# Raw inputs projected and scaled afterwards in three layers, new fillers, halved value steps, and another order of tree rows

## The reference

```python
def _layernorm(x, axis=-1, eps=1e-05):
    m = jnp.mean(x, axis=axis, keepdims=True)
    v = jnp.var(x, axis=axis, keepdims=True)
    return (x - m) / jnp.sqrt(v + eps)
# l0a: linear attention with rotation and biases
q = (x @ Wq + bq); k = (x @ Wk + bk); v = (x @ Wv + bv)
q = _rope_apply(q, cos, sin); k = _rope_apply(k, cos, sin)
# l1x: softmax attention over the context, with mask; l2x: the same without mask
# l1a: relu attention
qkv = jax.nn.relu(jnp.einsum('bnc,oc->bno', x, qkv_weight))
vk = jnp.einsum('bnhe,bnhd->bhed', v_pad, k)
vk_q = jnp.einsum('bhed,bnhd->bnhe', vk, q)
proj_input = vk_q[..., :D] / (vk_q[..., D:] + EPS)
# l1f: four binary trees of depth 8 route each token to a leaf of its own
h = act(jnp.einsum('bsd,bsdl->bsl', x, w1[leaf]) + b1[leaf])
out = jnp.einsum('bsl,bsld->bsd', h, w2[leaf]) + b2[leaf]
# l1f: q, k, v = tree(xn); att = softmax(q @ k.T / sqrt(D)); y = xn + att @ v; y + tree_f(y)
# l3x: 16 heads of 64
q = _split_heads(x @ w_q)
dots = jnp.einsum('bhid,bhjd->bhij', q, k) * scale
attn = jax.nn.softmax(dots, axis=-1)
```

## Time and profile before

| | us |
|---|---|
| runs | 518.43, 514.8, 518.2; median 518.2 |
| the profiled execution | 517.47 |
| its span | 515.7 |
| TensorE busy | 471.1 (91%) |
| VectorE busy | 330.1 (64%) |
| ScalarE busy | 239.2 (46%) |
| GpSimd busy | 66.7 (13%) |
| mean granted clock of TensorE | 0.977 |

### The profile page before, as it was taken

The page is one execution under the profiler, slowest core; times in us unless marked ns, Lnnn a source line. Parts: engine busy times, 40 slices in busy tenths (PEclk is TensorE's granted clock), DMA queues, the critical chain, the costliest instruction groups (busy, mean ns, idle before and its releaser), DMA issues.

```text
span 515.7 us, 10193 instructions
## 1 busy us (share of the span) xinstructions
PE 471.1 (91%) x4120; PEld 388.0 (75%) x4120; DVE 330.1 (64%) x815; ACT 239.2 (46%) x480; POOL 66.7 (13%) x149
## 2 busy tenths in 40 slices
PE   8988999999875869899989899889999999999897
PEld 6857885555664868656557779769899899999797
DVE  5666579984745836898335464376777777755644
ACT  7223546777400434666733246275566565532131
POOL 1220124000016020200014005500000000001000
PEclk9989999999898898999999999899999999999999
DMA  7908301910177734000019000000000000019000
GB/s 261 396 3 175 74 1 41 208 22 1 30 282 255 291 93 159 1 1 0 2 60 390 3 1 1 2 0 1 1 0 2 1 1 1 1 42 417 34 1 5
DMA packets 9070, 42.05 MB, mean 82 GB/s; under 512 B 2287, under 2 KB 4919, under 8 KB 6327
## 3 DMA queue, kind: packets, MB, share of 16 engines
q1 hardware_dynamic: 7297, 32.73, 19.5%
q0 software_dynamic: 1728, 8.68, 4.6%
HBM read 34.72 MB, written 0.08 MB: 67 GB/s over the span
## 4 chain that ended last, share of the span: by engine, by line
PE 61%; DVE 18%; DMA 7%; issue 6%; POOL 4%; ACT 3%; SPq 1%; POOLq 0%; DVEq 0%; ACTq 0%
PE banks L281 55%; PE banks L284 6%; DVE peaks L1566 4%; DMA p_const<-in_const 3%; DMA region<-in_tree_v,leaf_no 2%; DMA region<-in_tree_f,leaf_no 1%; DVE probs L1563 1%; DVE small L2559 1%; POOL mv L386 1%; DVE probs L634 1%; DVE nmax L633 1%; DVE nmax L630 1%; DVE xnT L399 1%; ACT probs L655 1%; SPq L307 1%
## 5 line engine op out<-in xcount | busy, mean ns | idle before, releaser
L281 PE MATMUL banks<-identb 128*128 128x128 bf16 x944 | 69.2, 230 | 8.4 <-DMA region<-in_tree_q,leaf_no 3.9
L281 PEld LDWEIGHTS banks<-identb 128*128 128x128 bf16 x944 | 63.3, 104 | 11.4 <-DMA region<-in_tree_q,leaf_no 4.1
L1566 DVE TENSOR_REDUCE peaks<-banks 128x1 f32<-128x1024 f32 x56 | 66.5, 1220 | 4.2 <-PE banks L281 3.1
L2559 DVE TENSOR_REDUCE small<-banks 128x1 f32<-128x1024 f32 x32 | 39.1, 1222 | 24.3 <-PE banks L281 24.1
L2653 ACT CAST weights_hi<-banks 128x512 fp32r<-128x512 f32 x64 | 35.0, 590 | 27.4 <-PE banks L284 23.4
L284 PE MATMUL banks<-p_first,probs 128*128 128x128 f32 x320 | 44.2, 275 | 3.5 <-ACT probs L658 1.7
L2644 ACT ACTIVATE probs<-banks,nmax 128x1024 f32<-128x1024 f32 x32 | 35.6, 1115 | 24.5 <-DVE nmax L2563 24.4
L2569 DVE TENSOR_TENSOR weights_lo<-banks,weights_hi 128x512 fp32r<-128x512 f32 x64 | 41.4, 683 | 7.4 <-ACT weights_hi L2653 7.4
L284 PEld LDWEIGHTS banks<-p_first,probs 128*128 128x128 f32 x320 | 36.4, 140 | 10.6 <-ACT probs L655 2.3
L1650 ACT ACTIVATE region<-banks,seen 128x512 f32<-128x512 f32 x64 | 37.9, 702 | 12.2 <-PE banks L281 12.2
L1650 ACT ACTIVATE region<-banks 128x512 f32<-128x512 f32 x64 | 33.4, 606 | 17.1 <-PE banks L281 16.7
(11 more groups left out here) (493 smaller groups left out, 907.6 us busy)
## 6 DMA issues: line engine op xcount, KB each, us to landing
region<-in_w_l2f SPq DMA_DIRECT2D x1, 4096.0 KB, 15.4
region<-in_w_l3f SPq DMA_DIRECT2D x1, 4096.0 KB, 13.5
region<-in_w_b SPq DMA_DIRECT2D x1, 3076.0 KB, 14.7
values<-in_ctx SPq DMA_DIRECT2D x2, 1024.0 KB, 7.9
region<-in_w_l0f SPq DMA_DIRECT2D x1, 2048.0 KB, 21.7
keys_l1x<-shared SPq DMA_DIRECT2D x8, 256.0 KB, 4.1
keys_l2x<-probsT SPq DMA_DIRECT2D x8, 256.0 KB, 5.1
region<-in_w_l3d SPq DMA_DIRECT2D x1, 2048.0 KB, 17.0
```

What stands on the lines that cost most here:

```text
L281: return nc.tensor.matmul(o, lhsT, rhs, start=start, stop=stop)
L1566: nc.vector.tensor_reduce(peaks[:, h // 4 % 2, i:i + 1], ps[:, 2 * a:2 * a + 2, :], AX.XY, ALU.max, negate=True).then_inc(VM.sem, VM.now(( ...
L2559: return nc.vector.tensor_reduce(small[:, half:half + 1], ps[:, 2 * half:2 * half + 2, :], AX.XY, ALU.max)
```

## The change

In **l0a, l1a and l3x** the raw x is transposed and projected, not the normalised one. The mean is taken out of the weights ahead of time: with center = 1/128 - identity, the product center x W is the centred weight with its sign turned (l0x centres the weights of l0a and l1a, l1f those of l3x). The scale 1/sqrt(var + eps) comes in behind the projection: as a factor in the bias additions of l0a, in the relus and in the quotient of l1a, and in l3x in the maximum's factor and the exponential's scale, now a column (`rooted`) where it was the number 0.125. `late_plan`, `late_vector` and `late_tensor` take the place of the three `start_` functions there.

**Fillers:** 18 go in l0x; l1a has 7 for 19; l3x has 9, 7, 6 and 9 for 20, 3, 3 and 5; l1f has 32 more ahead of tree q; l2x has 22 more ahead of its first turned shift and 20 behind it. **l0a** moves the second block of keys behind the projections. **l1x** splits each value step of four matmuls in two. **l1f** fetches the first layer of tree v ahead of k's second layer; VectorE computes the hidden units of v ahead of k's products, and the row maximum stands inside v's chain, after three of nine rows.

```diff
+        def late_vector(dve, tag, bias):
+            x = xs[:, x_at[tag], :]
+            vl(dve, nc.vector.bn_stats(st[:, :], x))
+            vl(dve, nc.vector.bn_aggr(mv[:, 0:2], st[:, :]))
+            nc.vector.tensor_scalar(mv[:, 2:3], mv[:, 1:2], EPS, None, ALU.add).then_inc(V.sem, V.now(tag + ".var"))
+            turn_vector(dve, tag + ".x0", xnT)
+            if bias is not None:
+                nc.vector.tensor_tensor(xb[:, :], x, bias, ALU.add)
+        def late_tensor(pe, tag, before):
+            turn_tensor(pe, tag + ".x0", xs[:, x_at[tag], :], before)
@@ l0x, TensorE, VectorE, ScalarE
-                fill(18)
+                loaded(pe, "w_a")
+                pe.wait_ge(V.sem, V.at("center"))
+                for i, w in enumerate(late_weights):
+                    mm(ps[:, 1 + i, 0:3 * P], center[:, :], w).then_inc(T.sem, T.now(("centred", i)))
                 pe.wait_ge(V.sem, V.at("l0x.prod"))
+                nc.vector.tensor_scalar(center[:, :], ident, 1.0 / P, None, ALU.subtract).then_inc(V.sem, V.now("center"))
+                for i, w in enumerate(late_weights):
+                    act.wait_ge(T.sem, T.at(("centred", i)))
+                    nc.scalar.copy(w, ps[:, 1 + i, 0:3 * P]).then_inc(A.sem, A.now(("centred", i)))
@@ l0a, TensorE, then VectorE
-                for b in (0, 1):
-                    keys_tensor(pe, "l1x", at["w_l1x_k"], b, 2 + b)
-                start_tensor(pe, tag)
+                pe.wait_ge(A.sem, A.at(("centred", 1)))
+                keys_tensor(pe, "l1x", at["w_l1x_k"], 0, 2)
+                late_tensor(pe, tag, "l0x.x")
                 distance_tensor(pe, 2)
...
                 m.then_inc(T.sem, T.now("l0a.qkv"))
+                keys_tensor(pe, "l1x", at["w_l1x_k"], 1, 3)
-                vl(dve, nc.vector.tensor_tensor(tG[:, :], src, bias, ALU.add))
+                vl(dve, nc.vector.scalar_tensor_tensor(tG[:, :], src, mv[:, 3:4], bias, ALU.mult, ALU.add))
@@ cross (l1x masked, l2x first)
-                early = {0: (key, 0), 1: (value, 0), 2: (value, 1), 3: (key, 1), 4: (key, 2), 5: (value, 2), 6: (key, 3),
-                         7: (value, 3)}
+                early = (((key, 0), (value, 0, 0)), ((value, 0, 1),), ((value, 1, 0),), ((value, 1, 1), (key, 1)),
+                         ((key, 2), (value, 2, 0)), ((value, 2, 1),), ((key, 3), (value, 3, 0)), ((value, 3, 1),))
                 if first:
                     peak(9)
+                    pe.wait_ge(VM.sem, VM.at((tag, 3, 0)))
+                    keep(22, 4)
                 turn(0)
-                if not first:
+                if first:
+                    keep(20, 4)
+                else:
                     peak(9)
@@ l1a
-                keep(16, 6)
-                start_tensor(pe, tag)
-                keep(3, 6)
-                pe.wait_ge(V.sem, V.at("l1a.xn.T"))
+                late_tensor(pe, tag, "l1x.x")
+                keep(7, 6)
+                pe.wait_ge(V.sem, V.at("l1a.x0.T"))
+                dve.wait_ge(G.sem, G.at("l1a.rstd"))
+                nc.vector.tensor_scalar(tB[:, :], ps[:, 1, 0:P], 0.0, mv[:, 3:4], ALU.max, ALU.mult)
@@ l1f, TensorE, VectorE, ScalarE, GpSimd
-                keep(44, 0)
+                keep(76, 0)
+                    mm(ps[:, 1 + i, :], center[:, :], wide_queries(i)).then_inc(T.sem, T.now(("l3x.wq", i)))
-                for n in "qk":
-                    tree_hidden(dve, n, tA[:, :])
-                    tree_products(dve, n)
+                tree_hidden(dve, "q", tA[:, :])
+                tree_products(dve, "q")
+                tree_hidden(dve, "k", tA[:, :])
                 tree_hidden(dve, "v", tA[:, :])
+                tree_products(dve, "k")
...
-                tree_chain(dve, "v", tree_bias("v"))
+                tree_chain(dve, "v", tree_bias("v"), largest)
+                    nc.scalar.copy(wide_queries(i), ps[:, 1 + i, :]).then_inc(A.sem, A.now(("l3x.wq", i)))
                 tree_gather_halves(pool, "k", "l1f.paths.even", "l1f.paths")
+                tree_gather_halves(pool, "v", "l1f.paths.even", "l1f.paths")
                 tree_gather(pool, "k", (2,))
-                tree_gather_halves(pool, "v", "l1f.paths.even", "l1f.paths")
@@ l3x, TensorE, VectorE, ScalarE
-                keep(20, 0)
-                start_tensor(pe, tag)
-                keep(3, 0)
-                pe.wait_ge(V.sem, V.at("l3x.xn.T"))
+                keep(9, 0)
+                pe.wait_ge(A.sem, A.at(("l3x.wq", 1)))
+                late_tensor(pe, tag, "l2f.x")
+                keep(7, 0)
+                pe.wait_ge(V.sem, V.at("l3x.x0.T"))
+                dve.wait_ge(G.sem, G.at("l3x.rstd"))
+                nc.vector.tensor_scalar(rooted[:, 0:1], mv[:, 3:4], 0.125, None, ALU.mult)
+                nc.vector.tensor_scalar(rooted[:, 1:2], mv[:, 3:4], -0.125, None, ALU.mult).then_inc(
+                    V.sem, V.now("l3x.rooted"))
-                                         bias=nmax[:, g:g + 1], scale=0.125,
+                                         bias=nmax[:, g:g + 1], scale=rooted[:, 0:1],
```

More of the change, by code:

```diff
@@ L832, in l0x @@
             start_plan(tag)
-            V.plan("l0x.q")
+            V.plan("l0x.q", "center")
             G.plan("prelude", "pairs", "wide")
@@ L846, in l0x @@
             V.plan("l0x.rd")
-            T.plan("l0x.rd")
+            T.plan("l0x.rd", ("centred", 0), ("centred", 1))
+            A.plan(("centred", 0), ("centred", 1))
             V.plan("l0x.prod")
@@ L998, in l0a @@
             tag = "l0a"
-            T.plan(*(("l1x", "kp", b) for b in (0, 1)))
-            start_plan(tag)
-            T.plan("d.2", "l0a.qkv", "mask.any", "d.3")
+            T.plan(("l1x", "kp", 0))
+            late_plan(tag)
+            T.plan("d.2", "l0a.qkv", ("l1x", "kp", 1), "mask.any", "d.3")
             V.plan("d.2", ("l1x", "low", 0), "l0a.v", "mask", "l0a.q", "l0a.k", "d.3")
@@ L1746, in tree_plan @@
                 V.plan(("h", n))
+            if first is not None:
+                V.plan(first)
             if n in "qk":
@@ L1836, in tree_products, with tree_chain @@
                     V.sem, V.now(("p", n, c)))
-        def tree_chain(dve, n, base):
+        def tree_chain(dve, n, base, between=None):
             h = units(n)
             for j in range(CHAIN):
+                if j == 3 and between is not None:
+                    between()
                 w = unit_rows(n, j)
@@ L1972, in l1f @@
             turn_plan("l1f.y")
-            T.plan("l1f.nodef", ("l2x", "vp", 0), "l1f.leaff", *(("l2x", "vp", b) for b in range(1, 4)))
-            A.plan(*(("l2x", "v", b) for b in range(4)))
+            T.plan("l1f.nodef", ("l2x", "vp", 0), "l1f.leaff", *(("l2x", "vp", b) for b in range(1, 4)), ("l3x.wq", 0),
+                   ("l3x.wq", 1))
+            A.plan(*(("l2x", "v", b) for b in range(4)), ("l3x.wq", 0), ("l3x.wq", 1))
             V.plan("l1f.turnf", "l1f.pathf.even", "l1f.pathf")
@@ L2019, in _ @@
                 values_tensor(pe, "l2x", at["w_b.l2x_v"], (2, 3, 4, 5), (1, 2, 3))
+                for i in range(2):
+                    if i:
+                        pe.wait_ge(A.sem, A.at(("l2x", "v", 0)))
+                    mm(ps[:, 1 + i, :], center[:, :], wide_queries(i)).then_inc(T.sem, T.now(("l3x.wq", i)))
                 tree_tensor(pe, "f")
@@ L2092, in _ @@
                 values_scalar(act, "l2x", (2, 3, 4, 5))
+                for i in range(2):
+                    act.wait_ge(T.sem, T.at(("l3x.wq", i)))
+                    nc.scalar.copy(wide_queries(i), ps[:, 1 + i, :]).then_inc(A.sem, A.now(("l3x.wq", i)))
                 tree_scalar(act, "f", CHAIN, LW)
```

75 lines of the change are left out of this document (45 added, 30 removed).

## The result

The changed kernel takes 519.62 us (median of 14 runs, 517.33 to 522.67). The kernel before takes 516.27 in 14 runs of its own, so the three runs shown ahead of the prediction (518.2) stood high. The ratio is 1.006, with a 95% interval of 1.0041 to 1.008: the change makes the kernel about 3.1 us slower (the medians are 3.35 apart). The prediction was 516.7, with a range up to 519.5.

What follows compares the result with a forecast made beforehand. The prediction gave TensorE 61% of the chain of waits. Its terms, -2.2 - 1.25 - 1.1 + 0.45 + 4.0 - 0.65 = -0.75 against 517.47, gave 516.7 us, with an 8-in-10 range of 511.3 to 519.5.

Steps and rivals of the forecast that it cites:

- The tree order in l1f: In l1f, v's units ahead of k's products: 4.0 us more, 2.9 at full clock, 4.8 if k's rows land late.
- the sum of k: In l1f, TensorE's 34 passes start at 177.1 after five us idle; one slow stretch adds 1.1, ending at 182.2.
- The first rival: In l1f, tree order pays: k's sum does not matter, v's earlier rows save 1.35 us; 511.3 us, chance 15%.
- The second: In l1f, k's rows land late, at 179.0, and the layer costs 2.5 us more: 519.2 us, chance 17%.
- The clock term of l3x: At l3x's start, a shorter TensorE gap removes a half-clock stretch: 1.25 us less, between 0 and 1.5.
- l2x: In l2x, 22 + 20 new fillers stand in TensorE's gaps: 0.65 us less; 0.9 more if 22 ran at half clock.
- l3x: Late normalisation in l3x: 1.36 + 1.25 - 0.1 - 0.3, net 2.2 us less.
- The third rival: In l3x and l2x, the clock does not come back, slow stretches only move: 518.9 us, chance 13%.
- l1x: In l1x, halved value steps make the eighth maximum later: 0.45 us more, 0 to 0.6.
- l1a and l0a: Late normalisation starts the projections earlier: l1a 1.25 us less (1.0 to 1.4), l0a 1.1 less (0.3 to 1.5).
- The fourth rival: In l0a, l1a and l3x, the power is waited for again at the evictions, so no time gained: 520 us, chance 5%.
- l0x: In l0x, centring matmuls of 1.3 us replace 18 fillers of 1.2 us: cost nothing.

Runs made afterwards that it cites:

- e2: Changed kernel with VectorE's l1f order as before, but the new order of fetches kept; 519.13 us, ratio 1.0069.
- e8: Kernel before with only the order of l1f changed (fetches, v's units, row maximum); 520.78 us, ratio 1.0098.
- e9: Changed kernel with l1f's fetches in the old order and VectorE still in the new one; 520.22 us, ratio 1.0088.
- e4: Changed kernel with whole instead of halved value steps in l1x; 518.41 us, ratio 1.0048.
- e3: Changed kernel with 84 fillers between q's sum and k's sum in l1f; 518.04 us, ratio 1.0042.
- e12: Kernel of e1 run again, unchanged; 515.74 us, ratio 0.9988 to the kernel before.
- e1: Changed kernel with the order of the trees in l1f as it was; 512.57 us, ratio 0.994 to the kernel before.
- e11: Kernel of e1 with whole value steps in l1x, all new fillers kept; 514.88 us, ratio 0.9983 to the kernel before.
- e6: Kernel of e1 without the 22 and 20 fillers of l2x; 513.37 us, ratio 0.9952 to the kernel before.
- e10: Kernel of e1 with whole value steps, no new l2x fillers and 44 instead of 76 fillers ahead of tree q; 513.34 us, ratio 0.997 to the kernel before.
- e7: Kernel of e1 with whole value steps, 16 fillers ahead of l1x's first turned shifts and l3x's second query_lo earlier; 513.6 us, ratio 0.9947.

## Why the prediction was wrong

**The tree order in l1f: right mechanism, size too small.** The step was the sum of k: VectorE's first product of k comes late, TensorE idles five us, the 34 passes start only there. The rows give an idle time of 5.08 and a sum that starts at 176.76, where I had 177.1. The term that failed is the length of the sum: I let one slow stretch fall in it and gave it 5.1 us, with 4.8 as the layer's worst; two fell back to back and the sum took 6.68. Two fell in e2, e8 and e9 as well, and only in e4 one. Even one was priced too low: with one the sum took 5.69 in e4, and the same 34 passes of q had taken 5.69 in the kernel before:

```profile
168.09 5.69 PE L281 MATMUL banks<-p_first,region 128*128 128x128 f32 x34 [1.81 <-issue]
```

The layer cost 5.2 in the profile, 5.0 in e8, and e3 took 3.0 of it back through the clock alone. Over all profiles, the new order gives l1f 55.4 to 56.3 us (changed kernel, e4, e8), the old one 49.8 to 53.1 in seven and 56.1 in e12; in the times e8 is 4.7 over the kernel before, and the changed kernel 7.0 over e1 and 3.9 over e12. So its cost is some 4 to 5 us by most of these numbers, and up to 7 by the pair of e1. The first rival (the tree order pays) is out: k's sum ended at 183.4, and that rival needed it before 178.5. The second (k's rows land late) is out as a cause: they landed at 176.0, ahead of the 177.3 from which it decides.

**The clock term of l3x.** I took 1.25 in l3x and 0.65 in l2x as clock regained, each against one execution that had seven slow stretches and a mean clock of 0.977, where the runs of that kernel have 0.983. A single execution is no base for such a gain. In the changed kernel's profile l2x gained 0.75 as forecast. In l3x the stretch went from the start and came back 16 us later, behind a wait of 1.65 that was there before as well (1.6, with no stretch behind it); l3x gained 1.0 in place of 2.2. It came in four of the ten profiles with that wait (changed, e4, e11, e12). In the other six (e1, e2, e3, e6, e9, e10) l3x gained 2.2 to 2.4, just the sum of its terms; there a slip in my sum (four more fillers at 0.06 are 0.25, not 0.1) is hidden by a start 0.16 faster than forecast (1.52 for 1.36). The third rival, the clock does not come back, priced at 2.15 and given 13%, is half right: in l2x it came back, in l3x not in this profile. The mean clocks of whole runs, 0.984 beside 0.983, can't decide it, since they hold the two stretches of k's sum; with the old order of trees and 76 fillers in l1f the runs have 0.986 to 0.992 (e1, e6, e7, e11, e12), where the kernel before has 0.982 to 0.983 beside them.

**l1x:** 0.45 forecast, 0.65 from the halved steps. Not forecast, and put at nothing without a reason, was the stretch behind the wait of 1.23 us ahead of the turned shifts, 0.78 before, which cost 1.1 (e2); with one at the layer's end, which the profile of before has too, l1x came to 1.8 in the profile.

**l1a and l0a:** 1.25 and 1.1 forecast, 1.28 and 1.2 measured. In l0a the number was met by luck: e8, with the old start, takes 0.6 less than before, 0.3 because VectorE waits 0.77 us for GpSimd's power and not 1.07, and 0.3 behind the projection, where before has a slow stretch and e8 none. So against e8 the new start gives 0.6. The fourth rival (the ladder only moves) is out; by its own terms its 520 should have read 520.6.

**l0x:** forecast nothing; the profile has 0.6 more. The profiles of the changed start give 25.4 to 26.1, and e8, with the old one, 25.90. So the centring matmuls show no cost that differs from the variation.

**The sum by terms:** against the forecast of -0.75 in the span, +3.2 came: l1f 1.2, l1x 1.4, l3x 1.2 and l0x 0.6 more than forecast, l0a, l1a and l2x 0.2 less, and the start and the untouched layers 0.2 less. Most of the miss is slow stretches that the sum left out or priced too low: those in the sum of k (1.6), the one in l3x (1.2) and the one in l1x (1.1). The profile of before stood 1.2 over the median of its 14 runs, 516.27, and that of the changed kernel 1.0 over its own, so the medians (3.35 apart) differ by about as much as the spans.

## What to carry over

Follow an input not only to the engine that waits for it, but to the longest piece of work that can start only behind it: VectorE's wait of 1.35 us for v's rows hid nothing, while k's rows fed four us of TensorE. Where an order opens a gap in TensorE, price the work behind the gap at half clock in full, and fill the gap if it must stay (e3 took back 3.0 us of the layer). Fillers are queued work too: the 76 ahead of q's sum kept its clock in most profiles and made it up to 3.5 us late in those where TensorE stopped among them. And count no gain from a slow stretch that one execution shows; of this kernel even medians of 12 runs came out 3 us apart for the same code.

## What the runs showed of the hardware

Three things I had not expected. First, which wait has a slow stretch behind it is not settled by the code. TensorE's wait of 3.7 to 4.1 us ahead of tree q had one behind it in all 14 profiles; the wait of 1.65 in l3x in four of ten; that of 1.23 in l1x in three of eight, with the same instructions up to there.

Second, during the gathers TensorE can stop with nothing in the profile to wait for, in e12 for 2.4 us between fillers and in e11 for 1.7, with the DMA engines 99 to 100% busy in e12. In e12 VectorE stopped too and went on in the same moments; in e11 it did not stop. (The idle time of 1.81 us marked "issue" in the kernel before is not such a stop: VectorE's first product of q starts at 167.34, and q's sum 0.75 us behind it, as in e10, where the profile names that product.)

The instructions come over DMA as well (the changed kernel's page lists a queue "instruction" with 33 packets and 0.54 MB), and the Trainium skill (Runtime: NRT & Kernel Launch, Instruction fetch mechanics) has each engine fetch its code by a DMA queue of its own, in blocks of 16 KiB, and calls this mostly hidden. A late block would fit stops under full queues, but e12's record of the DMA queues speaks against it (from 158 to 162 us, from 162 to 166, and the last two lines from 166 to 170):

```profile
q0 software_dynamic: 297, 1.35, 98.7%
q0 software_dynamic: 329, 1.56, 99.5%
q0 software_dynamic: 299, 1.66, 100.0%
q14 instruction: 1, 0.01, 0.5%
```

No instruction packet shows from 158 to 166 us, and the one behind it starts at 169.7, when TensorE had stopped four times and gone on four times. Whether the record holds every engine's fetches, no run shows, so the cause stays open.

Third, in eight of the 12 runs of e3 0.8 to 1.1 us more lie outside the span than in other kernels, and no run tells why.
